# Cross-attention and experts: two heads per 32-row group, single-width q and k projections, key spreading and both normalisations on GpSimd, context laid out transposed

## The reference

```python
q = (layernorm(x) @ Wq.T + bq)   # 16 heads of 16
k = (ctx @ Wk.T + bk); v = (ctx @ Wv.T + bv)
att = einsum('bhsd,bhtd->bhst', q, k) / sqrt(16)
att = where(pad_mask == 0, -1e9, att); att = where(subsq_mask == 0, -1e9, att)
x = x + einsum('bhst,bhtd->bhsd', softmax(att), v)
x = x + shared(layernorm(x)) + sum over the top 2 of 12 experts of w * expert(layernorm(x))
```

## Time and profile before

| what | value |
|---|---|
| runs of the kernel before | 658.15, 661.57, 663.26 us |
| median of the runs | 661.57 us |
| span of the profiled execution | 661.7 us |
| mean granted TensorE clock of it | 0.960 |
| instructions | 14825 |

### The profile page before, as it was taken

How to read it: one execution, slowest core, us unless ns; L and a number is a source line. 1 busy time by engine, 2 the same in 40 slices (tenths; PEclk the granted TensorE clock), 3 DMA queues, 4 the chain that set the end, 5 groups by cost and what they waited for, 6 DMA issues and landing times.

```text
span 661.7 us, 14825 instructions
## 1 busy us (share of the span) xinstructions
PE 601.9 (91%) x4406; PEld 508.4 (77%) x4407; DVE 460.1 (70%) x1037; ACT 302.4 (46%) x677; POOL 348.7 (53%) x403
## 2 busy tenths in 40 slices
PE   7899999998887876989999999999999999997893
PEld 6677878887767765778878888788887888787792
DVE  7888888979865547766666667666776666653575
ACT  4467676655654223434444444344443444432331
POOL 3891100110294673998884893888893860006361
PEclk9999999989987977989999999999999999999798
DMA  8957465248404323345643544445633311003242
GB/s 278 333 212 258 153 223 206 88 183 295 176 28 172 122 94 86 144 156 196 223 145 109 184 170 137 139 136 209 219 137 127 125 42 40 24 18 99 77 137 79
DMA packets 47910, 98.95 MB, mean 150 GB/s; under 512 B 4736, under 2 KB 23808, under 8 KB 47872
## 3 DMA queue, kind: packets, MB, share of 16 engines
q1 hardware_dynamic: 36192, 50.40, 21.5%
q0 software_dynamic: 10976, 47.72, 21.5%
q10 hardware_dynamic: 704, 0.33, 0.2%
HBM read 57.15 MB, written 39.19 MB: 146 GB/s over the span
## 4 chain that ended last, share of the span: by engine, by line
PE 68%; DVE 11%; issue 7%; ACT 6%; another core or an unknown queue 4%; POOL 3%; DMA 1%; DVEq 0%; ACTq 0%; SPq 0%; POOLq 0%
PE ps_s L801 27%; PE ps_o L834 9%; PE ps_o L835 5%; PE ps_s L763 5%; PE ps_t L586 3%; PE ps_t L811 3%; PE ps_t L515 2%; PE ps_x L515 2%; ACT prob L1006 1%; DVE nmax L1351 1%; PE ps_s L811 1%; PE ps_o L596 1%; PE ps_x L822 1%; PE ps_s L574 1%
## 5 line engine op out<-in xcount | busy, mean ns | idle before, releaser
L801 PE MATMUL ps_s<-ring,xTh 128*128 (+1 forms) x516 | 152.2, 417 | 1.4 <-DVE xTl L1674 1.4
L1850 POOL TENSOR_TENSOR ring<-stage,ring 128x512 fp32r<-128x512 f32 x80 | 100.6, 1290 | 1.2
L801 PEld LDWEIGHTS ps_s<-ring,xTh 128*128 128x128 f32 x516 | 88.5, 189 | 16.1 <-DVE xTl L1674 1.6
L834 PE MATMUL ps_o<-ring,hTh 128*128 x258 | 97.0, 413 | 2.2 <-DVE hTl L1669 2.2
L1660 DVE TENSOR_TENSOR ag<-ps_s,up_bias 128x512 f32<-128x512 f32 x129 | 88.8, 689 | 12.4 <-PE ps_s L801 10.0
L801 PE MATMUL ps_s<-ring,xTl 128*128 (+1 forms) x258 | 80.6, 393 | 0.0
L835 PE MATMUL ps_o<-ring,hTl 128*128 x258 | 72.8, 282 | 0.0
L1836 POOL TENSOR_TENSOR ve<-mv,eps 128x2 f32<-128x2 f32 x16 | 3.9, 246 | 130.6 <-DVE mv L1390 117.2
L2036 POOL DMA_INDIRECT gath<-rows_out,idx_out x32 | 30.9, 967 | 77.2 <-DMA rows_out<-y_row 57.0
L1130 ACT ACTIVATE ps_s<-ag 128x256 f32<-128x256 f32 x129 | 50.2, 389 | 39.0 <-DVE ag L1660 37.9
L1665 DVE TENSOR_TENSOR ag<-ag,ps_s 128x256 f32<-128x256 f32 x129 | 54.3, 421 | 16.1 <-ACT ps_s L1130 0.5
(11 more groups left out here) (272 smaller groups left out, 1350.7 us busy)
## 6 DMA issues: line engine op xcount, KB each, us to landing
rows_in<-y_row SPq DMA_DIRECT2D x8, 3328.0 KB, 12.2
stage<-in_w POOLq DMA_DIRECT2D x12, 1536.0 KB
stage<-in_w POOLq DMA_DIRECT2D x12, 768.0 KB, 5.4
up_bias<-in_bias POOLq DMA_DIRECT2D x12, 768.0 KB, 4.6
xrow<-rows_in SPq DMA_DIRECT2D x43, 128.0 KB, 2.1
rows_out<-y_row SPq DMA_DIRECT2D x43, 128.0 KB, 1.7
cbuf<-in_ctx SPq DMA_DIRECT2D x8, 256.0 KB, 2.9
xn_all<-xn2p SPq DMA_DIRECT2D x8, 256.0 KB
```

Source lines behind the costliest of these rows:

```text
L801: last = pe_.matmul(ps_s[:, i, :], x[:, c, :], weights(place, off + c * 2 * HR + i * 2 * D, 2 * D), start=n == 0, stop=n == 5)
L834: pe_.matmul(ps_o[:, :], hTh[i][:, c, :], weights(place, a, 2 * D), start=i == 0 and c == 0, stop=False)
L1850: last = pool.tensor_tensor(lo_ap[:, c:c + PIECE], src[:, c:c + PIECE], hi_ap[:, c:c + PIECE].bitcast(f32), ALU.subtract)
```

## The change

**What moves.** The weights `wq` and `wk` are held once (256 columns, in an order of heads such that the two heads of a 32-row group stand side by side), so q and k are one step each, `k` and `q`, of 12 matmuls. Two heads share 32 rows; to keep them apart POOL writes the keys twice (`spread_keys`), once with the odd head's rows zero and once with the even head's (`km_hi`, `km_lo`), and the scores multiply `q_hi` and `q_lo` by 256 columns that hold both. The context comes transposed from DRAM into `c_raw`, so `cT` goes, and POOL splits it (`split_ctx`). POOL also normalises x (`normalise_x`) and the rows (`normalise_rows`). The masks are one DVE operation each, with the large value carried by the identity that multiplies them. The conversion of the shared weights on POOL, once done before pair 0 ended, is spread over POOL's rounds 1 to 4. The values follow each set of transposes one by one instead of all together. A softmax unit now takes half of each of the four score banks instead of two whole banks. The second half of a pair on PE now ends: `xT`, fourth transposes, values, `r`, the last values, `l`, output transposes, scores of the next pair.

**Waits that are new.** `load_ctx(p+2)` waits for the split of the context before (`c_split`); the scores wait for `k_spread`; `ln1_stats(p+3)` waits for `xn1_ready`; the statistics of a residual wait for `xn2_ready`.

The diff, cut to its core:

```diff
-            def pair(p, par, first, last):
-                if first:
-                    sp.wait_ge(xb_ready, index_of("cT", p, first, last) + 1)
-                    load_ctx(2)
-                else:
+            def pair(p, first):
+
+                sp.wait_ge(c_split, p + 2)
+                load_ctx(p + 2)
+                if not first:
                     save_xn2(p - 1)
-                sp.wait_ge(xb_ready, index_of("cT", p, first, last, first) + 1)
-                load_ctx(p + 3)
                 fill(p + 1)
 
-            pair(0, 0, True, False)
-            with sp.Fori(0, (PAIRS - 4) // 2) as i:
-                pair(i * 2 + 1, 1, False, False)
-                pair(i * 2 + 2, 0, False, False)
+            pair(0, True)
+            with sp.Fori(1, PAIRS - 3) as p:
+                pair(p, False)
+            sp.wait_ge(c_split, PAIRS - 1)
+            load_ctx(PAIRS - 1)
             save_xn2(PAIRS - 4)
             fill(FILLS - 2)
...
-                elif s == "cT":
-                    pe.wait_ge(ctx_in, 16 * (pp + 1))
-                    last = transposes(ps, cbuf, 2)
-                elif s[0] in "qk":
-                    wh, wl, a = (wqh, wql, 0) if s[0] == "q" else (wkh, wkl, 1)
-                    for gg in parts:
-                        cols = slice((2 * int(s[1]) + gg) * P, (2 * int(s[1]) + gg + 1) * P)
+                elif s in "qk":
+                    wh, wl = (wqh, wql) if s == "q" else (wkh, wkl)
+                    hi, lo = (xTh1, xTl1) if s == "q" else (cTh[par], cTl[par])
+                    if s == "k" and 0 in parts:
+                        pe.wait_ge(c_split, pp + 1)
+                    for r in parts:
+                        cols = slice(r * P, (r + 1) * P)
                         n = 0
-                        for w, t in ((wh, aTh), (wh, aTl), (wl, aTh)):
+                        for w, t in ((wh, hi), (wh, lo), (wl, hi)):
                             for c in range(KC):
-                                last = pe_.matmul(ps[:, gg * 256:(gg + 1) * 256], w[:, c, cols], t[a][:, c, :],
+                                last = pe_.matmul(ps[:, r * 256:(r + 1) * 256], w[:, c, cols], t[:, c, :],
                                                   start=n == 0, stop=n == 5)
                                 n += 1
...
-                for g in range(4):
-                    for k in (k_hi, k_lo):
+                for r in range(2):
+                    for n, (q, k) in enumerate(((q_hi, km_hi), (q_lo, km_hi), (q_hi, km_lo))):
                         for j in range(4):
-                            last = pe_.matmul(ps_s[:, j, g * P:(g + 1) * P],
-                                              q_st[par][32 * j:32 * j + 32, g, b * P:(b + 1) * P],
-                                              k[par][32 * j:32 * j + 32, g, b * P:(b + 1) * P],
-                                              start=False, stop=g == 3 and k is k_lo)
+                            rows = slice(32 * j, 32 * j + 32)
+                            last = pe_.matmul(ps_s[:, j, r * 256:(r + 1) * 256].rearrange("p (a t) -> p a t", a=2),
+                                              q[par][rows, r, b * P:(b + 1) * P], k[par][rows, b, r, :, :],
+                                              start=False, stop=r == 1 and n == 2)
                 last.then_inc(scores_ready, 1)
...
                 for b in range(2):
                     vec.bn_stats(bn1[:, b, :], x_all[:, bass.ds((pp * 2 + b) * D, D)]).then_inc(ln1_bn, 1)
                 ve.wait_ge(ln1_bn, pp * 2 + 2)
+                if not (isinstance(pp, int) and pp == 0):
+                    ve.wait_ge(xn1_ready, pp)
                 vec.memset(tick[:, :], 0.0)
...
-                softmax_shift(p * 4 + 1, 1, p * 2, None if first else lambda: put("k0"))
-                put("k1")
+                    softmax_shift(p * 4 + 1, 1, p * 2)
+                    put("k")
+                    if isinstance(p, int) and p == PAIRS - 3:
+                        choose(0, 0)
+                    elif not isinstance(p, int):
+                        ln1_stats(p + 3)
+                    softmax_max(p * 4 + 2, 2, p * 2 + 1)
+                    norm(p - 1, 1)
+                    put("q")
+                softmax_add(p * 4 + 2, 2)
...
                 if b == 1:
                     ve.wait_ge(nstep, (p * 2 + b) * 2 + 2)
+                    if not (isinstance(p, int) and p == 0):
+                        ve.wait_ge(xn2_ready, p)
...
+            def split_ctx(q):
+                gp.wait_ge(ctx_in, 16 * (q + 1))
+                if q >= 2:
+                    gp.wait_ge(xb_free, index_of("v", q - 3, q == 3, False) + 1 if q > 2 else FIRST.index("v") + 1)
+                hi, lo = cTh[q % 2], cTl[q % 2]
+                pool.tensor_scalar(hi[:, :, :], c_raw[:, :, :], 1.0, 0.0, ALU.mult, ALU.add).then_inc(c_hi, 1)
+                gp.wait_ge(c_hi, q + 1)
+                pool.tensor_tensor(lo[:, :, :], c_raw[:, :, :], hi[:, :, :].bitcast(f32), ALU.subtract).then_inc(c_split, 1)
+            def normalise_x(q):
+                rstd(ln1_var, ln1_rs, mv1, ve1, rs1, q, pstep)
+                gp.wait_ge(ln1_rs, q + 1)
+                if q:
+                    gp.wait_ge(xb_ready, first_step("xT", q - 1) + 1)
+                for b in range(2):
+                    last = pool.tensor_scalar(xn1[:, b, :], x_all[:, (2 * q + b) * D:(2 * q + b + 1) * D], mv1[:, b, 0:1],
+                                              rs1[:, b:b + 1], ALU.subtract, ALU.mult)
+                last.then_inc(xn1_ready, 1)
+            def normalise_rows(q):
+                rstd(ln2_var, ln2_rs, mv2, ve2, rs2, q, pstep2)
+                gp.wait_ge(ln2_rs, q + 1)
+                if q:
+                    gp.wait_ge(xn2_saved, 16 * q)
+                    gp.wait_ge(xb_ready, index_of("r", q, False, False) + 1)
+                for b in range(2):
+                    last = pool.tensor_scalar(xn2p[:, b, :], x_all[:, (2 * q + b) * D:(2 * q + b + 1) * D], mv2[:, b, 0:1],
+                                              rs2[:, b:b + 1], ALU.subtract, ALU.mult)
+                last.then_inc(xn2_ready, 1)
+            def spread_keys(q):
+                idx, par = first_step("k", q), q % 2
+                gp.wait_ge(xb_hi, (HI_FIRST.index("k") if q == 0 else hi_index("k", q - 1, q == 1)) + 1)
+                for src, out in ((k_hi, km_hi[par]), (k_lo, km_lo[par])):
+                    if src is k_lo:
+                        gp.wait_ge(xb_free, idx + 1)
+                    for a, col in ((0, C_EVEN), (1, C_ODD)):
+                        last = pool.tensor_scalar(out[:, :, :, a, :].rearrange("p b r t -> p r b t"),
+                                                  src[:, :, :].bitcast(f32).rearrange("p r (b t) -> p r b t", b=2),
+                                                  const[:, col:col + 1], None, ALU.mult)
+                last.then_inc(k_spread, 1)
...
+            spread_keys(1)
+            split_ctx(2)
+            normalise_x(2)
+            for p in range(1, PAIRS - 1):
+                if p + 2 < PAIRS:
+                    split_ctx(p + 2)
+                    normalise_x(p + 2)
+                spread_keys(p + 1)
+                if p == 1:
+                    shared_up_hi()
+                if p == 2:
+                    shared_up_lo(0, W1S // 2)
+                if p == 3:
+                    shared_up_lo(W1S // 2, W1S)
+                if p == 4:
+                    shared_down()
+                    gp.wait_ge(converted, 1)
+                    load_raw1(0)
+                    load_raw2(0)
+                normalise_rows(p - 1)
+
+            gp.wait_ge(zero_out, 16 * FILLS)
+            gp.wait_ge(xn2_saved, 16 * 4)
```

501 lines of the change are left out of this document (217 added, 284 removed).

## The result

The changed kernel takes 698.9 us (median; 697.46 to 699.99), the kernel before 662.28 beside it: ratio 1.057, 95% interval 1.0535 to 1.0606. It is slower by more than the range of the prediction allowed (647 to 677). The profiled execution took 697.46 us, with a span of 695.6.

A forecast was written before the change was run, and what follows sets the result against it. The prediction took a ring of POOL's work and SP's queued context load to bound attention, with rounds of 24.3 us; an earlier last pair and later scatters, half of each, gave -0.5 us: 661 us, range 647 to 677.

The forecast's parts named there:

- What bounds the kernel before, and the work that TensorE and VectorE lose: Attention pairs of 22.7 us: PE nearly full, DVE close behind; PE needs 3 to 4.5 us less, DVE 4.2.
- My upper bound of 0.26: Scores on PE: each group of 256 columns takes between 0.13 and 0.26 us.
- The walk's 20.4 us a pair: Step through one attention pair: PE and DVE alone would allow 20.4 us in place of 22.7.
- The ring through SP's queue: Context load waits behind save and fill, which wait for POOL's rows: rounds of 24.3 us in attention.
- the price of POOL's operations with a scalar per partition: POOL's norms and key spreading: 0.64 us for 512 elements, 0.407 for 256; high end 1.27 for 512.
- key spreading over 4 us per pair: Sign on POOL that would show the prediction wrong; the sum had 2.5 us per pair.
- that the keys and the conversion lie beside VectorE's chain: POOL's keys and weight conversion, 5.1 us, run beside VectorE's chain of 5.7 us and don't lengthen the round.
- The start: Before pair 1: first scores some 3 us earlier, pair 1 at 41.5 us, rows of round 1 at 56.4.
- The end: Last pair's opening scores at 179.3 us (181.20 before), scatters about 1 us later; half of each taken, -0.5 us.
- rival 2: From context landing to round's end: the ring with dearer POOL work, +12 us, 673 us; chance 0.33.
- Rival 1: Attention pairs: context loads land in time, engines set pairs of 20.4 us, -14.5 us, 647 us; chance 0.23.
- Rival 3: Start of the experts: hangs on scatters and POOL's conversions, so halved projections don't show; 662 us; chance 0.07.

The follow-up runs named there:

- experiment 5: Changed kernel with the context loaded ahead of save and fill, and the router's steps r and l later in each pair: 669.2 us, ratio 1.0111.
- experiment 3: Changed kernel with immediates for POOL's scalars per partition (normalising, keys' zeroing left out) and the context loaded ahead of save and fill: 653.3 us, ratio 0.990.
- experiment 12: Kernel of experiment 10, with POOL's split of the next context waiting for the pair's first transposes: 623.8 us, ratio 0.9886.
- experiment 1: Changed kernel with immediates in place of POOL's scalars per partition, leaving out normalising and the zeroing of the other head's keys: 667.4 us, ratio 1.0114.
- experiment 7: Changed kernel with the keys spread by ScalarE (hi) and VectorE (lo) instead of POOL, nothing else: 686.9 us, ratio 1.0379.
- experiment 9: Changed kernel with eight matmuls of zeros in TensorE's wait for xn2p: 673.1 us, ratio 1.0662 in a session with a faster kernel before.
- experiment 8: Changed kernel with norms on VectorE, keys on ScalarE and VectorE, context loaded ahead, router's steps later, VectorE's start tables behind x's first split: 664.9 us, ratio 1.0045.
- experiment 4: Changed kernel with immediates for the key spreading only, the zeroing of the other head's keys left out: 681.4 us, ratio 1.0325.
- experiment 6: Changed kernel with both norms back on VectorE, nothing else: 685.5 us, ratio 1.0359.
- experiment 10: Kernel of experiment 8 with three matmuls of zeros a pair on TensorE: 628.7 us, ratio 0.9954.
- experiment 11: Kernel of experiment 10 with the router's steps early and the three matmuls of zeros ahead of the wait for xn2p: 648.2 us, ratio 1.0272.

## Why the prediction was wrong

**What bounds the kernel before, and the work that TensorE and VectorE lose:** right in kind, a little too large. In rounds at full clock TensorE is busy for 19.3 us (experiment 5) instead of 21.9, which is 2.6 less where I had 3 to 4.5; VectorE is busy for 15.8 instead of 19.3, 3.5 less where I had 4.2. The score groups of 256 columns came out at the low end of my bounds; six groups follow one another by 0.12 us at full clock (timeline of TensorE, kernel after):

```profile
116.48 0.39 PE L568 MATMUL ps_s<-km_hi,q_hi 32*128 32x256 f32 x4
116.71 0.29 PE L568 MATMUL ps_s<-km_hi,q_lo 32*128 32x256 f32 x4
116.82 0.29 PE L568 MATMUL ps_s<-km_lo,q_hi 32*128 32x256 f32 x4
...
117.40 0.65 PE L597 MATMUL ps_o<-const,outT 128*128 128x128 f32 x4
```

From the first group to the next work it is 0.92 us, against 1.05. My upper bound of 0.26 was far off. The Trainium skill (TensorE: Matmul & The Clock Gate, "Measured speedup vs the span model") gave an estimate of 0.15 by its factor of 3.07 for four matmuls on 32 rows each (its row is for 512 columns). The trace's 0.12 is shorter: a group of four takes no longer than one of the projection's matmuls of 256 columns, two of which take 0.24 us (113.13 to 113.37). The measurement decides. The walk's 20.4 us a pair for the engines alone was reached within 0.5 to 0.6 us by the best rounds of experiments 3 and 12.

**The ring through SP's queue:** right in place and size. From the end of a round to the context on POOL I had 12.9 us; POOL's waits in rounds 2 to 5 were 12.8 to 14.0. Opening it alone was worth 2.3 points.

**The step that failed: the price of POOL's operations with a scalar per partition.** The prediction took 0.64 us for 512 elements and 0.407 for 256, "as these have one tensor input", with 1.27 as the high end. They take 1.57 and 1.22 to 1.24. That is 3.7 us a round for the keys (6.2 instead of 2.5) and 3.3 for the two norms (four times 0.82): 7.0 us. The true price lies above the operation with two tensor inputs, which I had taken for a bound because a second input seemed the dearest thing that could be added. The prediction had named its own sign of being wrong, "key spreading over 4 us per pair", and that is what happened. With the price put back, and all else kept, the kernel takes 1.0114 of before (experiment 1), and its rounds are those of the prediction within 1.7 us.

**A second step fell with it: that the keys and the conversion lie beside VectorE's chain.** They did at my price, 5.1 beside 5.7. At the true one keys and conversion are 8.7 us, so POOL's own work took the place of VectorE's chain and set the round. With the measured prices my walk gives 27.5 us for VectorE's branch (27.9 in experiment 7) and 30.5 for POOL's (30.7 in round 3). Because POOL and not VectorE closed the ring, the trace shows the wait that I had named as a sign, VectorE at the statistics of x until POOL's xn, but at only 2.27 us in round 3 and of no consequence. The ring had two parallel branches, and repairing one leaves the other: experiment 7 gained 1.9 points, not 5.

**The start:** wrong by 12 us. I had put the first scores some 3 us earlier, and they came later, at 20.40 against 18.55 before; the rows of round 1, put at 56.4, were ready at 68.66. The same price did it in part, norm and key spreading of pairs 0 to 2 in series on POOL: with immediates that point came at 59.5, 9 us sooner. The remaining 3 us are other waits, and I have not separated them.

**The end:** the scores that open the last pair, put at 179.3, came at 224.80 (181.20 before). I had carried half of the change in attention into the total; of the 44 us there 34 reached the span.

**The rivals:** rival 2, the ring with dearer POOL work, was the right one, place and sign, and its chance of 0.33 was too low; its 673 us was too little, since the bound that it used was. Rival 1 was what opening the ring gives, but only with the norms and keys cheap as well (experiment 3). Rival 3 did not happen. The Trainium skill's "roughly line-rate" for one-input operations on GpSimd (GPSIMD Engine Reference, "Engine selection") agrees with 0.62 us for 512 elements with immediates, and not with 1.57 for a tile of the same size with a scalar per partition; the measurement decides.

**TensorE's clock** was no term of the sum. In the changed kernel it fell to 0.80, and raising it to 0.89 gained nothing (experiment 9); in experiment 8 its fall cost some 4 us.

What stays open: why experiments 4 and 6 gained some 10 us less than the sums of their parts. For experiment 6 half of it lies behind attention. The rounds 2 to 5 of the two (26.2 to 30.4 and 26.4 to 30.8 us) come with clocks of 0.78 to 0.88 and 0.73 to 0.94, and no run separates that. The part behind the save of round 6 takes 475 to 487 us from kernel to kernel in the first sessions, although the change does not touch it; that is open too.

## What to carry to other kernels

Where a change puts a form of operation on an engine that the trace does not show there, such as a scalar per partition instead of an immediate, the nearest other form is no bound: leave the top of the range open, or price it by itself first, above all where the operation stands in a ring. Name every branch of a ring, since a repair of one is worth only the distance to the next. And when an engine is relieved, look at what its gaps do: TensorE's clock can fall to half after short waits one after another. Matmuls of zeros in them went with the full clock in experiments 10 and 12, but not in 11, so read the granted clock again after each move.
